# A graph attention layer's softmax sums: which engine adds which tiles, and head 0's row

## What is computed

```python
g = jnp.einsum('bcn,bnm->bcm', fea, Wg)                  # fea = x transposed
g = jax.nn.relu(g * para.reshape(1, C, N))
q = jnp.transpose(g, (0, 2, 1)).reshape(B, N, h, hd)...   # 4 heads of 64
kv = (x @ kv_w) ...                                       # keys and values
attn = jax.nn.softmax(jnp.einsum('bhnd,bhmd->bhnm', q, k) * scale, axis=-1)
out = jnp.einsum('bhnm,bhmd->bhnd', attn, v)
x = _layernorm(x + out)                                   # end of layer 0
```

## Time and profile before

| | before |
|---|---|
| median of 3 runs | 2901.39 us |
| the profiled execution's own time | 2902.2 us |
| its span, first to last instruction | 2900.2 us |
| TensorE busy | 2735.8 us, 94% |
| VectorE busy | 1982.4 us, 68% |
| ScalarE busy | 1657.1 us, 57% |
| GpSimd busy | 1276.2 us, 44% |
| mean granted TensorE clock | 0.976 |

### The profile page before, as it was taken

One profiled execution on the slowest core, in us unless ns is written; L12 is line 12 of the kernel. 1 busy time (PEld: TensorE's weight loads), 2 busy tenths in 40 slices (PEclk: granted clock), 3 DMA queues, 4 the chain that ended last, 5 costly groups with the idle time before them and its releaser, 6 DMA issues. The chain is left out here.

```text
span 2900.2 us, 39341 instructions
## 1 busy us (share of the span) xinstructions
PE 2735.8 (94%) x12436; PEld 1850.9 (64%) x12436; DVE 1982.4 (68%) x2843; ACT 1657.1 (57%) x2146; POOL 1276.2 (44%) x684
## 2 busy tenths in 40 slices
PE   7999999999999999999999999998699999989964
PEld 5565665656656565665656656564588888878854
DVE  6787786877868687786877868685533333338878
ACT  6566575766657666575766657664422222227768
POOL 3755647565475756647575575746200000000015
PEclk9999999999999999999999999999799999999985
DMA  4123222232222223222232222220323222305556
GB/s 138 59 82 104 76 72 73 72 101 84 72 76 77 75 80 99 82 72 67 78 95 89 72 76 72 80 61 27 116 102 116 87 87 91 109 18 197 186 230 256
DMA packets 128223, 276.21 MB, mean 95 GB/s; under 512 B 12208, under 2 KB 62384, under 8 KB 124592
## 3 DMA queue, kind: packets, MB, share of 16 engines
q1 hardware_dynamic: 128176, 275.62, 29.6%
HBM read 178.79 MB, written 62.98 MB: 83 GB/s over the span
## 5 line engine op out<-in xcount | busy, mean ns | idle before, releaser
L304 POOL TENSOR_TENSOR psum<-psum,probs 128x1024 f32<-128x1024 f32 x320 | 783.6, 2449 | 149.9 <-ACT probs L372 130.6
L372 ACT ACTIVATE probs<-sc_ps 128x1024 f32<-128x1024 f32 x512 | 505.6, 1023 | 419.8 <-PE sc_ps L815 367.1
L544 DVE TENSOR_REDUCE mx<-mx_ps 128x1 f32<-128x512 f32 x768 | 521.6, 690 | 318.0 <-PE mx_ps L784 316.2
L831 PE MATMUL pv_ps<-probs,v 128*64 128x512 f32 x2048 | 492.4, 604 | 0.0
L815 PE MATMUL sc_ps<-qa,ka 128*128 128x512 f32 x1024 | 387.2, 404 | 0.0
L815 PE MATMUL sc_ps<-qb,kb 128*128 128x512 f32 x1024 | 381.0, 395 | 0.5
L784 PE MATMUL mx_ps<-ka,qa 128*128 128x512 f32 x768 | 316.8, 423 | 8.7 <-DVE mx L544 3.1
L831 PEld LDWEIGHTS pv_ps<-probs,v 128*64 128x64 f32 x2048 | 125.7, 136 | 224.5 <-issue 194.1
L815 PEld LDWEIGHTS sc_ps<-qa,ka 128*128 128x128 f32 x1024 | 187.8, 188 | 105.5 <-issue 64.1
L1170 DVE TENSOR_TENSOR agg_lo<-ag_ps,agg_hi 128x1024 fp32r<-128x1024 f32 x32 | 39.2, 1225 | 313.5 <-ACT agg_hi L1097 313.4
L784 PEld LDWEIGHTS mx_ps<-ka,qa 128*128 128x128 f32 x768 | 140.1, 187 | 173.2 <-issue 77.9
(11 more groups left out here) (194 smaller groups left out, 5557.6 us busy)
## 6 DMA issues: line engine op xcount, KB each, us to landing
adj_ring<-in_adj_dram SPq DMA_DIRECT2D x128, 512.0 KB, 3.7
pre_scratch<-pre SPq DMA_DIRECT2D x28, 1024.0 KB, 4.5
pre<-pre_scratch SPq DMA_DIRECT2D x28, 1024.0 KB, 4.9
x<-in_x_dram SPq DMA_DIRECT2D x16, 1024.0 KB, 5.6
kb<-ka SPq DMA_DIRECT2D x64, 256.0 KB, 3.3
qa<-qa SPq DMA_DIRECT2D x64, 256.0 KB, 3.1
res<-in_x_dram SPq DMA_DIRECT2D x16, 1024.0 KB, 5.6
x_scratch<-res SPq DMA_DIRECT2D x16, 1024.0 KB, 4.5
```

The costliest lines, as they stand in the source:

```text
L304: pool.tensor_tensor(psum[:, h % 2, :], probs[:, 0, :] if k == 1 else psum[:, h % 2, :], probs[:, k % PR, :], ALU.add).then_inc(s["pool_ad ...
L372: nc.scalar.activation(probs[:, i % PR, :], sc_ps[:, t % 2, :], ACT.Exp, scale=SCALE)\
L544: nc.vector.tensor_reduce(mx2[:, nh, n:n + 1], mx_ps[:, nh, :], AX.X, ALU.max)\
L831: ins = nc.tensor.matmul(pv_ps[nh * HD:(nh + 1) * HD, h % 2, :], v[:, i, h * HD:(h + 1) * HD], probs[:, i % PR, nh * BANK:(nh + 1) * BANK] ...
```

## The change

GpSimd no longer adds tiles 0 and 1. VectorE does (`add_first`, one 128x1024 add of `probs` 0 and 1 into `psum`), once the second exponential of the head is done; GpSimd then adds tiles 2 to 7, six adds as before, and `add_last` is gone. `sum_up` waits for GpSimd's sixth add, the exponentials of tiles 4 and 5 for VectorE's add. On VectorE `add_first(b, h)` stands behind the first four half maxima of the next head; for head 3 it stands behind `weigh(b+1, 1)` and `xt_low(b+1, 0)`.

With it go three changes of order: `k_low(b, 2)` and `k_low(b, 3)` move from between head 0's maxima to behind its row; head 0's line of `MAX_HALVES` changes, so that two halves of head 1's maxima stand ahead of part 1 of tile 0's scores; and in `g_product` `sum_up` moves from the middle of step n = 1 to its end.

```diff
--- before.py
+++ after.py
@@ -65,10 +65,11 @@
     SG = P // 4
     SN = N // 4
     SQ = SN // P
-    MAX_HALVES = [[[0, 1, 1], [2, 1, 1, 1, 1], [2, 1, 1, 1, 1], [1, 1, 0, 0, 0]]] + \
+    MAX_HALVES = [[[2, 1, 1], [1, 1, 1, 1, 0], [2, 1, 1, 1, 1], [1, 1, 0, 0, 0]]] + \
         2 * [[[0, 1, 1, 1, 1], [1, 1, 1, 1, 0], [2, 1, 1, 1, 1], [1, 1, 0, 0, 0]]]
     SUM_PAIR, DEN_PAIR, BACK_PAIR = 1, 2, 3
     POOL_ADDS = T - 2
+    FIRST_TILES, LAST_TILES = range(0, 2), range(2, T)
 
     x_v = x.rearrange("b (p t) c -> b p t c", t=T)
     res_v = x.rearrange("b (t p) c -> b p t c", p=P)
@@ -144,7 +145,7 @@
             "rowT_ready",
             "xth_done", "abs_done", "tanh_done", "whi_done", "kh_done", "qh_done", "v_evac", "exp_done",
             "xhi_done", "x_split", "xtl_done", "w_done", "wlo_done", "kl_done", "qt_done",
-            "ql_done", "qr_done", "max_done", "merged", "row_done", "pool_added", "acc_done", "sum_ready", "rden_done",
+            "ql_done", "qr_done", "max_done", "merged", "row_done", "first_added", "pool_added", "sum_ready", "rden_done",
             "copied_out", "den_copied", "denT_ready", "back_ready", "res_added", "stats_done", "mv_done", "veps_done", "rstd_done", "res_done")}
         adj_in = [sem(f"adj_in{i}") for i in range(AR)]
         qa_in = [sem(f"qa_in{h}") for h in range(HEADS)]
@@ -294,15 +295,13 @@
                     wait(pool, s["x_split"], b + 2)
                 wait(pool, s["ql_done"], 4 * b + 4)
                 for h in range(HEADS):
-                    for k in range(1, POOL_ADDS + 1):
-                        done = POOL_ADDS * (4 * b + h) + k - 1
-                        if k == 1:
-                            wait(pool, s["sum_ready"], 4 * b + h - 1)
-                        else:
-                            wait(pool, s["pool_added"], done)
+                    for k in range(2, T):
+                        wait(pool, s["pool_added"], POOL_ADDS * (4 * b + h) + k - 2)
+                        if k == 2:
+                            wait(pool, s["first_added"], 4 * b + h + 1)
                         wait(pool, s["exp_done"], 32 * b + 8 * h + k + 1)
-                        pool.tensor_tensor(psum[:, h % 2, :], probs[:, 0, :] if k == 1 else psum[:, h % 2, :],
-                                           probs[:, k % PR, :], ALU.add).then_inc(s["pool_added"], 1)
+                        pool.tensor_tensor(psum[:, h % 2, :], psum[:, h % 2, :], probs[:, k % PR, :], ALU.add)\
+                            .then_inc(s["pool_added"], 1)
 
             split_x(0)
             pool.wait_ge(s["x_split"], 1)
@@ -363,12 +362,12 @@
                 wait(act, s["st_ready"], 32 * b + t + 1)
 
                 wait(act, s["pv_done"], 32 * b + t + 1 - PR)
-                if i < PR - 1:
-                    wait(act, s["pool_added"], POOL_ADDS * (4 * b + h - 1) + i + PR)
-                elif i == PR - 1:
-                    wait(act, s["acc_done"], 4 * b + h)
+                if i < PR:
+                    wait(act, s["pool_added"], POOL_ADDS * (4 * b + h - 1) + i + PR - 1)
+                elif i < PR + 2:
+                    wait(act, s["first_added"], 4 * b + h + 1)
                 else:
-                    wait(act, s["pool_added"], POOL_ADDS * (4 * b + h) + max(1, i - PR))
+                    wait(act, s["pool_added"], POOL_ADDS * (4 * b + h) + i - PR - 1)
                 nc.scalar.activation(probs[:, i % PR, :], sc_ps[:, t % 2, :], ACT.Exp, scale=SCALE)\
                     .then_inc(s["exp_done"], 1)
 
@@ -554,12 +553,11 @@
                 src = (mx_ps if h else sc_ps)[0:T, 0, 0:P]
                 nc.vector.tensor_scalar(row[:, :], src, -1.0, None, ALU.mult).then_inc(s["row_done"], 1)
 
-            def add_last(b, h):
-
-                wait(dve, s["exp_done"], 32 * b + 8 * h + 8)
-                wait(dve, s["pool_added"], POOL_ADDS * (4 * b + h + 1))
-                nc.vector.tensor_tensor(psum[:, h % 2, :], psum[:, h % 2, :], probs[:, (T - 1) % PR, :], ALU.add)\
-                    .then_inc(s["acc_done"], 1)
+            def add_first(b, h):
+                wait(dve, s["exp_done"], 32 * b + 8 * h + 2)
+                wait(dve, s["sum_ready"], 4 * b + h - 1)
+                nc.vector.tensor_tensor(psum[:, h % 2, :], probs[:, 0, :], probs[:, 1, :], ALU.add)\
+                    .then_inc(s["first_added"], 1)
 
             def invert_sums(b, h):
                 wait(dve, s["denT_ready"], 4 * b + h + 1)
@@ -593,8 +591,6 @@
             def body(b, last):
 
                 before = not isinstance(b, int) or b > 0
-                if before:
-                    add_last(b - 1, HEADS - 1)
                 weigh(b, 4)
                 w_low(b, 3)
                 weigh(b, 5)
@@ -614,20 +610,19 @@
                     moments(b - 1)
                 q_times_para(b, 0)
                 q_times_para(b, 1)
-                maxima(b, 0, range(0, 4))
+                maxima(b, 0, range(T))
+                maxima_row(b, 0)
                 k_low(b, 2)
-                maxima(b, 0, range(4, 5))
                 k_low(b, 3)
-                maxima(b, 0, range(5, T))
-                maxima_row(b, 0)
-                maxima(b, 1, range(T))
+                maxima(b, 1, FIRST_TILES)
+                add_first(b, 0)
+                maxima(b, 1, LAST_TILES)
                 maxima_row(b, 1)
 
                 for h in (1, 2):
-                    maxima(b, h + 1, range(0, 1))
-                    add_last(b, h - 1)
-                    maxima(b, h + 1, range(1, 4))
-                    maxima(b, h + 1, range(4, 7))
+                    maxima(b, h + 1, FIRST_TILES)
+                    add_first(b, h)
+                    maxima(b, h + 1, range(2, 7))
                     invert_sums(b, h - 1)
                     maxima(b, h + 1, range(7, T))
                     maxima_row(b, h + 1)
@@ -635,10 +630,11 @@
                     if h == 2 and not last:
                         weigh(b + 1, 0)
 
-                add_last(b, 2)
                 if not last:
                     weigh(b + 1, 1)
                     xt_low(b + 1, 0)
+                add_first(b, 3)
+                if not last:
                     w_low(b + 1, 0)
                     xt_low(b + 1, 1)
                     weigh(b + 1, 2)
@@ -667,7 +663,6 @@
                 .then_inc(s["consts_set"], 1)
             dve.wait_ge(s["consts_set"], 4)
             over_batches(dve, B, body)
-            add_last(B - 1, HEADS - 1)
             invert_sums(B - 1, HEADS - 1)
             add_head(B - 1, HEADS - 1)
             row_stats(B - 1)
@@ -751,9 +746,9 @@
                                                        start=n == 0 and k == 0, stop=n == T - 1 and k == 2)
                         if n == T - 1 and c == 0:
                             ins.then_inc(s["g_first"], 1)
-                        if before and n == 1 and c == 0:
-                            sum_up(b - 1, HEADS - 1)
                     ins.then_inc(s["g_step"], 1)
+                    if before and n == 1:
+                        sum_up(b - 1, HEADS - 1)
                     if before and n == 2:
                         transpose_sums(b - 1, HEADS - 1)
                     if before and n == 3:
@@ -835,7 +830,7 @@
 
             def sum_up(b, h):
 
-                wait(pe, s["acc_done"], 4 * b + h + 1)
+                wait(pe, s["pool_added"], POOL_ADDS * (4 * b + h + 1))
                 wait(pe, s["copied_out"], 4 * b + h + 1)
                 for g in range(4):
                     ins = nc.tensor.matmul(pv_ps[g * SG:(g + 1) * SG, h % 2, 0:SN], ones[:, :],
```

## The result

The changed kernel takes 2916.03 us (median of 5 runs, 2915.67 to 2917.72) against 2902.35 (5 runs, 2900.33 to 2903.39). The ratio is 1.0049, 95% interval 1.0037 to 1.0061: slower by 13.7 us, where 10.6 had been forecast. The profiled execution spans 2915.7 us, before 2900.2; it is the slowest of the five (2917.72).

A forecast was written before the change was run, and what follows sets the result against it. TensorE's own order bounds the kernel, busy 122.12 of 124.62 us a batch. Batches 1 to 15 add 1.48 - 0.89 = 0.59 each (8.9), batch 0 1.05, the end 1.2: 11.1 in total, 2912 us; range 2906 to 2918 (0.60).

The forecast's parts named there:

- `sum_up`: In `g_product`: TensorE's wait for `add_last` goes, saving 1.06 us and the restart, 1.15, before part is given back.
- What is given back: In `g_product`: later `den_copy` delays VectorE's chain, TensorE waits 0.3 us for `w_low(6)`; shift at head 0's first score tile 0.46.
- Tile 7 and the copy of v: Head 0's row: the 0.81 us wait before tile 7 goes, but `v_copy(b, 0)` lets only 0.35 be kept, plus 0.08.
- Head 0's stretch: From head 0's first score matmul to `values`: grows from 6.78 to 8.26 us, by 1.48, with `add_first` among the maxima.
- Heads 1 to 3: `add_first` in the later heads fits VectorE's idle time or replaces another add: zero cost.
- The lock: Rival, 0.08: GpSimd's sixth add still runs at `add_first` in heads 1 and 2, costing up to 2.4 us each; 2946.
- The end: End of the last batch: one more GpSimd add of 2.4 us replaces VectorE's 1.22, costing 1.2.
- The sum: Whole kernel: batches 1 to 15 each 0.59 us longer, batch 0 1.05, the end 1.2; total 11.1 us.
- cancellation: Rival, 0.15: head 0's stretch grows by only 0.8 to 1.2 us, the early copy wait partly hidden; about 2903.
- the absorbed add: Rival, 0.17: VectorE's add costs nothing in head 0, growth zero, so faster: 2889, or 2879 with nothing given back.

The follow-up runs named there:

- e4_adds_only: The changed kernel with all three changes of order undone, so the adds alone are exchanged: 2905.68 us, ratio 1.0010 to the kernel before.
- e10_after_den: The changed kernel with `den_copy` behind the distance and tanh of step 5 on ScalarE: 2907.32 us, ratio 1.0011 to the kernel before.
- e8_klow_only: The kernel before with only the `k_low` edit, both `k_low` behind head 0's row: 2895.97 us, ratio 0.9975.
- e1_late3: The changed kernel with head 0's `add_first` behind six half maxima instead of four: 2892.9 us, ratio 0.9966 to the kernel before.
- e2_late4: The changed kernel with head 0's `add_first` behind eight half maxima instead of four: 2898.61 us, ratio 0.9985 to the kernel before.
- e5_late3_mid: e1_late3 with `sum_up` back in the middle of step 1 of `g_product`: 2882.83 us, ratio 0.9929 to the kernel before.
- e6_late3_mid_old: e5_late3_mid with the old line of `MAX_HALVES` for head 0: 2880.29 us, ratio 0.9922 to the kernel before.
- e3_halves_old: The changed kernel with the old line of `MAX_HALVES` for head 0: 2907.97 us, ratio 1.0017 to the kernel before.

## Why the prediction was right, point by point

- **`sum_up`.** Forecast 1.15 saved at first. In e4_adds_only and e10_after_den it is all there at tile 0: 26.03 to 24.88. GpSimd's sixth add ends 3.17 after the batch's start, 1.7 later than the 1025.3 of the forecast, since two of its adds take 3.2 (one starts at 1029.02, the next at 1032.33); that was allowed for, and TensorE comes 2.5 after it.
- **What is given back.** Forecast shift at tile 0 0.46 (the prediction's own places, 1049.89 and 1049.4, give 0.49), measured 0.49; through ScalarE's queue, as forecast (e10_after_den). The wait for `w_low(6)` was forecast at 0.3 and is 0.19, and step 6 stands 0.81 earlier, not 0.75. The other 0.32 goes where the forecast had it: VectorE, now without idle time, starts `q_times_para` only 0.31 earlier (1054.66), and tile 0, at 1057.11, follows a `q_high` that ends at 1056.98.
- **Tile 7 and the copy of v.** Forecast 0.43 of 0.81 kept, measured 0.44 in e8_klow_only. First scores 0.91 earlier, forecast 0.89.
- **Head 0's stretch.** Forecast 6.78 to 8.26, measured (medians) 6.74 to 8.39. This is the term that was mis-sized: 1.65 instead of 1.48, 0.17 in each of the fourteen steady batches, 2.4 us, most of the 3 us by which the total came out above the forecast. The early halves start at 1.38, forecast 1.28, and the add starts 0.11 after its exponential ends (1076.11, 1076.22), where I took 0.05 for each release; it ends at 6.15, forecast 6.0. The order of the waits was as forecast, with half 6 at 6.80 against 6.68. The growth stands at the upper edge of the 1.25 to 1.65 that was given, near the 1.6 for slower releases. The remaining 0.04 is the choice of batch: the one of the earlier trace rows has 6.78, the median 6.74.
- **Heads 1 to 3.** Forecast no change; h1 to h2 is 20.61 in both. The lock stayed out: in the changed kernel's trace GpSimd's sixth add has ended 0.9 us before head 1's `add_first` and 1.3 before head 2's; in e1_late3 0.26 before head 1's, and in e2_late4 it has not.
- **The end.** GpSimd's sixth add is waited for 2.31 at the end of the last batch, `add_last` was for 1.19 there: 1.1 more, forecast 1.2.
- **The sum.** Steady batches are 0.75 longer, forecast 0.59. The rivals: cancellation and the absorbed add did not occur, and e1_late3 shows what the second would have looked like.

The profiled executions differ by 15.5, more than the medians. About 1.1 of that lies in batch 0 before head 0 and another 1.1 behind the last `sum_up`, in the second layer. In both places the program does the same work in both kernels; see the last section.

Not tried: the new line of the table in the kernel before by itself. Beside the add behind six halves it costs 0.15 of stretch (e5_late3_mid against e6_late3_mid_old). Nor was the add moved in heads 1 to 3, where it costs nothing.

## What to carry to other kernels

Here VectorE takes half maxima in lockstep with TensorE: of the two PSUM buffers, each must be read before TensorE fills it again. In that stretch VectorE's add of 1.23 us cost TensorE 1.06 (e3_halves_old) to 1.52 (the changed kernel against e1_late3). The same add two halves later, in the time in which TensorE does `values`, cost nothing (e6_late3_mid_old). So before an operation is moved to a less busy engine, look at that engine's idle gaps at the very place, not at its share of the span. And when a wait goes, look at once at what stands behind the waiting engine's next release: here 0.65 of 1.15 was lost because a copy on a third engine stood in front of work that did not need it.

## What the runs showed of the hardware

The granted clock falls to its half level, 1.2 of 2.4 GHz, once near the start of the kernel, and when it comes back differs from profile to profile, although the program is the same up to there. TensorE idles for 5.3 us until about 36.5 us and is then busy; the clock falls in the idle time (0.93 in the window 30.00:36.60 of the changed kernel, 0.75 in that of the kernel before). The windows behind it (clock in the column behind POOL), in the changed kernel:

```profile
36.60:40.00 3.40, 3.40 (x8) 2.72 (x9) 3.07 (x3) 3.37 (x4) 0.00 (x0) 0.50 0.77 233
40.00:42.60 2.60, 2.60 (x7) 2.00 (x7) 2.17 (x3) 2.28 (x3) 0.00 (x0) 0.52 0.23 90
```

in the kernel before:

```profile
36.60:40.00 3.40, 3.40 (x8) 2.72 (x9) 3.25 (x3) 3.37 (x4) 0.00 (x0) 0.50 0.75 234
40.00:42.60 2.60, 2.60 (x12) 2.06 (x12) 1.99 (x3) 2.57 (x3) 0.00 (x0) 0.97 0.21 82
```

and in e10_after_den:

```profile
36.60:40.00 3.40, 3.40 (x10) 2.69 (x11) 3.36 (x4) 3.37 (x4) 0.00 (x0) 0.60 0.79 251
40.00:42.60 2.60, 2.60 (x13) 2.15 (x12) 1.87 (x2) 2.57 (x3) 0.00 (x0) 1.00 0.16 60
```

In all three the half level reaches into TensorE's busy time, furthest in the changed kernel, where the second window has 7 matmuls instead of 12 or 13. Batch 0's `g_product` is over at 53.08 in the changed kernel, at 51.98 in the kernel before and at 51.53 in e10_after_den. From the last `sum_up` to the end, in the second layer, it takes 884.0 in the changed kernel, 882.9 before and 880.8 in e10_after_den; what makes that difference was not looked into. So each of the two places moves by 1 us or more that no edit made, and the line of the table is worth only 2.5 us in the end (e5_late3_mid against e6_late3_mid_old). Small differences are better read from the steady batches, which agree within 0.2 us in the kernel before and in the changed one.
